# Attention of a two-layer network: P V with V stationary and P transposed moving, two heads in one PSUM bank

## The reference, cut to what matters

```
xn = layernorm(x) * gamma + beta
q, k, v = heads(xn @ w_qkv.T + b_qkv)            # 8 heads of 64
pos = heads(pe @ w_pos.T)
score = (q + u_bias) k^T + (q + v_bias) pos^T
attn = softmax(score * 64 ** -0.5)               # 345 x 345 for each head
out = concat(attn @ v) @ w_out.T + b_out
```

## Time and profile before

| | us |
|---|---|
| runs: median (lowest to highest) | 3003.32 (2994.98 to 3011.47) |
| profiled execution: span, first to last instruction | 2993.0 |
| median of the runs less that span | 10.3 |
| PE matmul busy | 2429.7 (81%) |
| DVE busy | 1541.5 (52%) |
| ACT busy | 698.7 (23%) |

### The profile page before, as it was taken

One profiled execution on the slowest core, in us unless ns is written; L12 is line 12 of the kernel. 1 busy time (PEld: TensorE's weight loads), 2 busy tenths in 40 slices (PEclk: granted clock), 3 DMA queues, 4 the chain that ended last, 5 costly groups with the idle time before them and its releaser, 6 DMA issues. The chain is left out here.

```text
span 2993.0 us, 50876 instructions
## 1 busy us (share of the span) xinstructions
PE 2429.7 (81%) x17112; PEld 1799.3 (60%) x17112; DVE 1541.5 (52%) x4738; ACT 698.7 (23%) x1812; POOL 724.5 (24%) x610
## 2 busy tenths in 40 slices
PE   0503999999999999999999999999999999845661
PEld 0302676767676767676767676767677776633340
DVE  1210446565656465646474747474747464643441
ACT  1100222232323232313131313132323232302120
POOL 0000000303030304040404040404040404146886
PEclk9956999999999999999999999999999999967775
DMA  4700000101010101010000000000000000005674
GB/s 127 263 29 30 8 12 9 44 9 40 9 33 9 30 9 27 9 24 9 19 9 18 9 22 9 18 9 18 9 19 9 18 9 12 4 6 109 117 115 64
DMA packets 122647, 100.95 MB, mean 34 GB/s; under 512 B 60273, under 2 KB 116511, under 8 KB 121836
## 3 DMA queue, kind: packets, MB, share of 16 engines
q0 software_dynamic: 51904, 40.97, 7.1%
q1 hardware_dynamic: 68290, 54.06, 6.6%
q10 hardware_dynamic: 2200, 2.57, 0.3%
HBM read 71.57 MB, written 67.84 MB: 47 GB/s over the span
## 5 line engine op out<-in xcount | busy, mean ns | idle before, releaser
L641 PE MATMUL Cb<-y_hi,wc_hi 128*128 128x345 f16 x1984 | 623.1, 314 | 70.1 <-DVE zneg L1164 70.1
L641 PE MATMUL Cb<-y_hi,wc_lo 128*128 128x345 f16 x1984 | 622.0, 313 | 0.0
L641 PE MATMUL Cb<-y_lo,wc_hi 128*128 128x345 f16 x1984 | 621.3, 313 | 0.0
L569 POOL TENSOR_TENSOR rstd<-ve,minus_half 115x3 f32<-115x3 f32 x64 | 54.8, 857 | 1957.3 <-DVE ve L1201 1409.3
L581 POOL DMA_INDIRECT slots_dram<-rows,slot_i x384 | 452.3, 1178 | 133.8 <-issue 133.8
L1036 ACT ACTIVATE Pm<-W,nmax 115x345 f32<-115x345 f32 x384 | 211.2, 550 | 607.3 <-DVE nmax L1376 607.2
L641 PE MATMUL W<-x_hl,w_hl 128*128 128x345 f16 x1536 | 290.5, 315 | 32.3 <-DVE KP L1360 17.4
L641 PEld LDWEIGHTS Cb<-y_hi,wc_hi 128*128 128x128 f16 x1984 | 196.6, 99 | 192.5 <-DVE zneg L1164 70.4
L641 PE MATMUL W<-KP,qv 128*115 128x345 f32 x768 | 300.6, 473 | 0.8 <-issue 0.8
L641 PE MATMUL Ob<-qv,PT 115*115 115x64 f32 x2304 | 282.3, 259 | 17.8 <-DVE PT L1384 10.0
L641 PEld LDWEIGHTS Ob<-qv,PT 115*115 115x115 f32 x2304 | 263.4, 181 | 22.7 <-DVE PT L1384 12.1
(11 more groups left out here) (196 smaller groups left out, 2970.9 us busy)
## 6 DMA issues: line engine op xcount, KB each, us to landing
band<-band_dram SPq DMA_DIRECT2D x68, 182.1 KB
slots_dram<-in_empty_slots POOLq DMA_DIRECT2D x1, 12352.0 KB
wc_hi<-slots_dram SPq DMA_DIRECT2D x64, 193.0 KB
qv<-in_wc SPq DMA_DIRECT2D x8, 992.0 KB, 10.3
slots_dram<-rows,slot_i POOLq DMA_INDIRECT x384
x_win<-in_xpad SPq DMA_DIRECT2D x17, 248.0 KB
x_T<-in_xTp SPq DMA_DIRECT2D x17, 188.0 KB
band_dram<-lg SPq DMA_DIRECT2D x17, 182.1 KB
```

Of the source, the lines that this page charges most:

```text
L569: pool.tensor_tensor(rstd[g][:, :], ve[g][:, :], minus_half[:, :], ALU.pow)\
L641: return pe.matmul(o, l, r, start=start, stop=stop)
```

## The change

Every unit's `Pm` is normalised before it is transposed: DVE takes the reciprocal of one column of sums for each unit, and ACT multiplies `Pm` in place (a new ACT operation on 115 x 345 for each unit, signal `scaled`). T moves from one step after S to two steps after S. `Pm` has three buffers in place of two, and `PT` holds three heads. PV is done once for two heads, at steps 8, 14, 20 and 26: V is stationary (115 x 64), the transposed P moves (345 columns), the one head's result goes to partitions 0 to 63 of the bank, the other's to 64 to 127. The bank is then already the transposed output, so one DVE copy for each pair puts it into `OT`; the 12 transposes, their three ACT copies and the multiplication by the reciprocals are gone.

```diff
+PAIRS = H0 // 2
+PAIR_UNITS = 2 * J
+def pair_at(s, after):
+    p, r = divmod(s - after, PAIR_UNITS)
+    return p if r == PAIR_UNITS - 1 and 0 <= p < PAIRS else None
...
-        Pm = sb("Pm", [A, 2, TOK])
-        PT = sb("PT", [A, 2, TOK])
+        Pm = sb("Pm", [A, 3, TOK])
+        PT = sb("PT", [A, 3, J, TOK])
...
-                for s in range(UNITS + 2):
+                for s in range(UNITS + 3):
...
-                    if 1 <= s <= UNITS:
-                        u = s - 1
-                        pe.wait_ge(p_ready.h, p_ready.at(b, u + 1))
+                    if 2 <= s <= UNITS + 1:
+                        u = s - 2
+                        pe.wait_ge(scaled.h, scaled.at(b, u + 1))
                         step(b, ("T", u), lambda w: turn_p(w, u))
...
+                    g = pair_at(s, 3)
+                    if g is not None:
...
                         for i in range(J):
-                            last = mm(Ob[o][0:A, j * DH:(j + 1) * DH], PT[:, u % 2, i * A:(i + 1) * A],
-                                      V[:, i, h * DH:(h + 1) * DH], start=(i == 0), stop=(i == J - 1))
+                            for r in range(2):
+                                h = 2 * g + r
+                                last = mm(Ob[o][r * DH:(r + 1) * DH, 0:TOK], V[:, i, h * DH:(h + 1) * DH],
+                                          PT[:, h % 3, i, :], start=(i == 0), stop=(i == J - 1))
...
-                pe.wait_ge(o_ready.h, o_ready.at(b, H0))
-                for j in range(J):
...
-                    for c in range(4):
-                        last = pe.transpose(W[i][:, c * A:(c + 1) * A], O[:, j, c * 128:(c + 1) * 128], ident[0:A, 0:A])
...
+                    if 1 <= s <= UNITS:
+                        u = s - 1
+                        act.wait_ge(prec_ready.h, prec_ready.at(b, u + 1))
+                        act.activation(Pm[:, u % 3, :], Pm[:, u % 3, :], ACT.Copy, scale=prec[:, u // J, u % J:u % J + 1])\
+                            .then_inc(scaled.h, scaled.up())
...
+                    if 1 <= s <= UNITS:
+                        u = s - 1
+                        dve.wait_ge(p_ready.h, p_ready.at(b, u + 1))
+                        dve.reciprocal(prec[:, u // J, u % J:u % J + 1], psums[:, u // J, u % J:u % J + 1])\
+                            .then_inc(prec_ready.h, prec_ready.up())
                     if s < UNITS:
                         conv_out(nb, 3 + s)
                         late(lb, s)
...
-                        link(dve.reciprocal(prec[:, h, :], psums[:, h, :]))
...
+                        dve.tensor_copy(OT[:, g, :], Ob[i][:, 0:TOK]).then_inc(o_ready.h, o_ready.up())
```

More of the change, by code:

```diff
@@ L93 @@
           + [("v", j) for j in range(J)] + unit_steps()
-          + [("oT", j) for j in range(J)] + [("out0", 0)]
+          + [("out0", 0)]
           + [("ln", 2), ("gate0", 0)] + [("hid", n) for n in range(2 * E0)]
           + [("sg", 0), ("su", 0), ("sg", 1), ("su", 1)])
-O_USES = [("O", h) for h in range(H0)] + [("Y", e) for e in range(E0 + 1)]
+O_USES = [("O", p) for p in range(PAIRS)] + [("Y", e) for e in range(E0 + 1)]
 C_USES = [("conv", o) for o in range(OC)] + [("w2", 0)]
@@ L126 @@
 FREED |= {("T", u): (("pt_ready_scalar", "pt_ready_vector")[u % 2], u // 2 + 1) for u in range(UNITS)}
-FREED |= {("oT", j): ("oT_ready", j + 1) for j in range(J)}
 FREED |= {("hid", n): ("hid_ready", n + 1) for n in range(2 * E0)}
 FREED |= {(w, c): ("hid_ready", 2 * E0 + c + 1) for w in ("sg", "su") for c in range(2)}
-FREED |= {("O", h): ("o_ready", h + 1) for h in range(H0)}
+FREED |= {("O", p): ("o_ready", p + 1) for p in range(PAIRS)}
 FREED |= {("Y", e): ("y_added", e + 1) for e in range(E0 + 1)}
@@ new lines, in present @@
+                    g = pair_at(s, 3)
+                    if g is not None:
+                        u = s - 3
+                        o, was, nth = freed(("O", g))
+                        if was:
+                            pe.wait_ge(was.h, was.at(b, nth))
+                        for v in u - 1, u:
+                            ready = (pt_ready_a, pt_ready_d)[v % 2]
+                            pe.wait_ge(ready.h, ready.at(b, v // 2 + 1))
+                        for i in range(J):
+                            for r in range(2):
+                                h = 2 * g + r
+                                last = mm(Ob[o][r * DH:(r + 1) * DH, 0:TOK], V[:, i, h * DH:(h + 1) * DH],
+                                          PT[:, h % 3, i, :], start=(i == 0), stop=(i == J - 1))
+                        last.then_inc(o_full[o].h, o_full[o].up())
@@ L1026, in present @@
                     tok_exp(tb)
-                for s in range(UNITS + 1):
+                for s in range(UNITS + 3):
                     if s < UNITS:
@@ L1040, in present @@
                         conv_out(nb, 3 + s)
[L1041 removed]
+                    if 1 <= s <= UNITS:
                         u = s - 1
+                        act.wait_ge(prec_ready.h, prec_ready.at(b, u + 1))
+                        act.activation(Pm[:, u % 3, :], Pm[:, u % 3, :], ACT.Copy, scale=prec[:, u // J, u % J:u % J + 1])\
+                            .then_inc(scaled.h, scaled.up())
+                    if 2 <= s <= UNITS + 1 and (s - 2) % 2 == 0:
+                        u = s - 2
                         i, nth = W_AT[("T", u)]
                         act.wait_ge(w_full[i].h, w_full[i].at(b, nth))
[L1045 to L1051 removed]
+                        pt_used(act, b, u)
+                        act.activation(pt_of(u), W[i][0:A, 0:TOK].rearrange("p (i a) -> p i a", i=J), ACT.Copy)\
+                            .then_inc(pt_ready_a.h, pt_ready_a.up())
                 p = 3 + UNITS + 4
@@ L1368, in present @@
                 turn_to(step_main, b)
-                for s in range(UNITS + 3):
+                for s in range(UNITS + 4):
                     if s < UNITS:
```

76 lines of the change are left out of this document (25 added, 51 removed).

## The result

The changed kernel takes 3099.10 us (3097.07 to 3104.14), the kernel before 3005.82 us over its four runs: ratio 1.0323 [1.0297, 1.0349], 3.2% slower. Predicted were 3057, in a range from 2978 to 3105. The profiled execution has a span of 3098.0 us against 2993.0: +105 us. Every listed run is 1.6 to 1.8 us longer than its span (3099.65 against 3098.0), so the profiled execution of before stands at about 2994.7, at the lower end of its runs (2994.98 to 3011.47). The medians differ by 93 us; the rest of the 105 is this spread of the old kernel, which no trace here explains.

A forecast was written before the change was run, and what follows sets the result against it. PE was taken to bound the kernel, DVE not far behind. Middle batch: 10.4 us idle less 6.7 work plus 0.5 clock; fourteen give 59, first -2, last +1, overlap -4: +54, 3057 us (2978 to 3105).

The forecast's parts named there:

- (e): Behind the end of attention: PE's drop to 1.2 GHz comes in all batches, not every second; +0.5 us a batch.
- 2.0 us a pair: New PV, halves fully paired: 8.0 us a batch against 13.5; with O's turning gone, 6.7 us of work saved.
- my estimate from the rule: PV weight loads for the same rows lie open: 0.6 us a pair, 2.3 us a batch; not taken whole.
- (a): Start of attention: the first T waits for the second exponential and its scaling; +0.3 us a batch.
- (b): Unit 5: PE's late matmul of unit 6 waits for DVE's late step, held by conv_out; +2.3 us a batch.
- (c): Units 15 to 21: DVE's full queue makes PE wait before T(15), T(16), T(17), T(21); +4.1 us a batch.
- (d): End of attention: waits before T(22), T(23) and last PV, 5.3 us against 1.9; +3.4 us a batch.
- the 4 us that I took off for overlap: Whole run: 4 us off the sum of 58, since a (c) wait overlaps a (d) wait when DVE runs late.
- more low clock: Rival: waits in (c) and (d) bring one more 3.4 us stretch at 1.2 GHz a batch; 3081 us, chance 0.12.
- PE busy falls by some 100 us: Sign to look for: PE's busy time over the run falls by some 100 us.
- The halves ran paired: Answers the rival that PV's array halves run in turn: 1.8 us a pair more, 3140 us, chance 0.07.
- PE did not stay the bound: Answers the rival that DVE keeps up at units 15 to 23, PE staying the bound: 2955 to 2989 us, chance 0.19.

The follow-up runs named there:

- e11: The kernel before, only its filler matmuls moved: more ahead of the first T, 14 before T(23) and the last two PV; first chunk ends at unit 5: 2929.90 us.
- e7: Changed kernel with e4's order, ACT also copying odd T from unit 15, and filler moved into waits at start, units 15 to 17 and end: 2922.49 us.
- e2: Changed kernel without the normalisation: no reciprocals or scalings, T waits for the exponential, still two steps behind S: 3019.25 us.
- e4: Changed kernel, queues reordered: DVE's reciprocal before T's copy, late step before conv_out; ACT scales before both; unit 23's reciprocal and scaling in its own step: 3045.16 us.
- e3: Changed kernel plus 25 filler-like matmuls a batch, results unread, before T(22), T(23) and the last PV: 3051.06 us.
- e8: The kernel before plus each unit's reciprocal and scaling, three Pm, T and PV one step later; old PV and turning of O kept: 3103.20 us.
- e12: e7 with three filler matmuls instead of four at units 3 to 14, and 13, 13, 6 instead of 9, 7, 5 at units 15 to 17: 2923.83 us.
- e1: Changed kernel with a pair's six PV matmuls reordered, three of one head and then three of the other: 3145.63 us.

## Why the prediction was right, and where not

The direction and the mechanism were right, the size fell short by 42 us, and one term was far too small: the clock, (e). By its own steps, for a middle batch:

- **PV.** "2.0 us a pair": 1.89 (962.14 to the next S at 964.03), its records starting in pairs, 0.29 us from pair to pair. At full clock PV and the turning of O went from 14.9 us (e11) to 7.6 (e7): 7.3 us, predicted 6.7. T took 0.8 us back, which I hadn't costed: its records take 0.117 us each in e7, 0.106 in e11. I left the Trainium skill's rule ("TensorE: Matmul & The Clock Gate", Part 3, The mechanism), that loads for the same rows do not run under matmuls, out of the sum. The trace agrees with leaving it out: with my estimate from the rule a pair would take 2.0 + 0.6 = 2.6 us, and 1.89 leaves no room for open loads.
- **(a) the start**, +0.3: 2.56 against 2.24: +0.32.
- **(b) unit 6**, 2.3: 2.05.
- **(c) T(15), T(16), T(17), T(21)**, 1.7, 1.3, 0.6, 0.7: 1.52, 1.14, 0.29, 0.71. The stretch from the maximum of unit 15 to that of unit 23 was to take 21 to 22 us: 979.16 to 1001.40, 22.2. e2 shows that most of (b) and (c) is DVE's queue, not the scaling.
- **(d) the end**, 3.1, 1.3, 0.9: 2.99, 0.58, 0.70. "T(22) about 2.8 us after the maximum of unit 23": 1001.40 to 1004.39, 2.99. e4 shows the part that the order of the queues has in T(22)'s wait (1.78 in its place). The sum of the end is another matter: with the other order (e4) and without the scaling (e2) it is still 3.92 and 3.95 us, since the last PV then waits for DVE's copy.
- **(e) the clock, +0.5: the step that failed.** e3 keeps the end at 2.4 GHz and has a stage 3.3 us longer than before (73.0 against 69.7): what waits and work come to without that clock, and I had 3.7. The low clock adds the other 3.6 us (76.6 against 73.0), seven times my term; it is rather more, up to 4.5, since e3's extra matmuls and what is left of its waits take 13.6 us where the changed kernel stood idle for 12.7. I had foreseen one stretch of 3.4 us in each batch. There are two, one of them 6.8 or 10.2 us long, over T(22), T(23), the last PV and the filler behind. In place of +4.2 a batch it was +6.9 in these two batches, and 6.75 on the mean of the fourteen.
- **The whole.** Trace against trace, 105 us where I had 54. The fourteen middle batches took 94.5 us more, from first S to first S, where I had 59: 36 of the 51 us that are missing, nearly all of them the clock. The first batch took 2.4 us more, where I had 2.1 less; the last, with all that lies behind it, 8.6 more, where I had 1; and the 4 us that I took off for overlap don't show. The 10.3 us that I put around the span were not around it: 1.65 are, the rest is the distance from the execution that was profiled to the median. Only because of that does the sum miss the changed kernel by 42 us and not by 51.

My rival "more low clock" priced just one such stretch more (3081) and gave it 0.12; it was the truth and still too cheap. What I missed is in the numbers that I had: a wait of 3.1 us and two more behind it, in 5 us, in place of three under 0.75 us each. The stage of before had shown what the milder case costs, and I took its price for the harsher one. "PE busy falls by some 100 us" failed for the same reason (23 us); at equal clock it holds: 2331.1 us in e7, 2427.1 in e11.

One reason of mine was only half of it, though it did no harm to the sum. I told the waits as what comes up once PE is relieved. Of the 8.4 us of added waits e2, with the relief and without the chain, has 6.1 (10.4 against 4.3), and e8, with the chain and without the relief, has 3.5: 1.67 at unit 6, 0.86 before T(16), and at the end 2.51 in place of 1.86. Either brings waits by itself. In time it comes out otherwise: the chain costs 98 us with the old PV (e8) and 80 with the new (3019 to 3099), while PV turned round, with its later T, costs 14 without the chain (e2, 3019, against 3005) and is worth 4 with it (3103 to 3099). So the scaling is the dear part, and what PV saves is used up by waits in either case. T comes a step later in e2, in e8 and in the changed kernel; what that alone does, no run shows. The halves ran paired, and PE did not stay the bound: those rivals fall.

## What to carry to other kernels

Price the waits of a change, then look whether there is independent work that can be moved into them; and give the kernel before the same treatment before crediting the change. Here the filler was worth 74 us on the old kernel, and by itself the change cost 93. The change on top of the filler, with the queues reordered and ACT copying more, was worth 6 to 7 us (e12 and e11, timed on the same chip, differ by 6.1, and their runs do not overlap). The waits at the end of this attention cost more than themselves, since what followed ran at half clock: 25 useless matmuls in them won 48 us.

The fastest version is e7 (2922.5 us, 2.7% faster than before); e11, at 2929.9, is nearly as good with nothing changed but a table.

## What was not expected of the hardware

By the profile's records, matmuls for different halves of the array's columns need not start in program order, though I wrote ahead of the prediction that every engine runs its list strictly in order. In e1 the seventh record (the other half) started 0.64 us after the first, with three of the first six still to come. The two records at 973.62 and 973.63 can't be of one head, whose records are 0.29 us apart. The Trainium skill, "TensorE: Matmul & The Clock Gate", Part 3, The mechanism (under "What overlaps and what doesn't"), has matmuls start and end strictly in program order; the measurement differs for the starts, and decides. Whether this is the array or the profile's records of it, no run here tells apart, but the 46 us between 3099 and 3146, in place of the 81 to 111 that I had expected of heads in turn, speak for the array. Two whole 64-column halves on the same 115 rows ran fully side by side: twelve records of 345 columns, float32, in 1.89 us, where one matmul of 345 columns, float32, on 115 of the array's columns gives two records in 0.63 us.
